# Two attention layers and two expert layers on one core: four groups of two heads in a turn of the loop instead of two

## The chip, the cores and the metric

The kernel runs on one core of a Trainium2 chip. The metric is the device time of one execution in microseconds (us). Before the change, three timed runs took 4503.47, 4507.40 and 4507.76 us, so the median is 4507.4 us. One further execution was profiled; it took 4508.5 us, and its trace spans 4506.7 us from the first to the last instruction.

## The reference, cut to what matters

The input x has 1024 rows of 128 numbers, and the context has 6404 rows of 128. Two layers follow each other, and each is a cross attention with 16 heads of 64 and then a mixture of 8 experts:

```python
x = x + tanh(g_xattn[0]) * xattn0(ctx, layernorm(x), mask, ...)   # keys: context and the 1024 rows; rmsnorm of q and k
x = x + tanh(g_ffn[0])   * moe0(layernorm(x), ...)
x = x + tanh(g_xattn[1]) * xattn1(layernorm(x), ctx, ...)         # keys: context and one null key
x = x + tanh(g_ffn[1])   * moe1(layernorm(x), ...)
# in each attention: softmax(q k^T) v for every head, then the output matrix
```

Nearly all the work is in the two attentions: 1024 queries against 7428 keys in the first and 6405 in the second, for every head.

## The kernel before

The kernel is written by hand for the five engines: each engine has its own list of instructions, and semaphores alone order them between engines. PE (TensorE) multiplies, ACT (ScalarE) exponentiates and copies, DVE (VectorE) forms the low parts of split numbers and adds outputs up, POOL (GpSimd) computes a few small roots, and SP (SyncE) issues the transfers.

`attention_layer` runs once for each of the two layers. The 16 heads go in `NG = 8` groups of `GH = 2` heads. Within a group the keys go in tiles of 128, which stand in ten chunks (59 tiles in the first layer, 51 in the second); each chunk is gone through twice, once for each half of the queries. One such step is one tile of keys by 512 queries by two heads. Steps go in pairs `i = 0 .. NPR - 1`, 59 and 51 pairs for a group.

In each pair PE computes the scores of two steps that lie ahead (L1114, three products for a split of 32-bit numbers into a high and a low part), then the outputs of the two present steps from the high part of the probabilities (L1132) and from the low part (L1139). ACT takes the exponential of the scores (`exp`, L638 in the first layer, L642 in the second), and DVE subtracts the high part from it (`p_low`, L797). Between these stand the projection of later tiles of keys and values (`project_kv`, L1049; `transpose_k`, L1057), what ACT and DVE make of it (`read_kv`, L607 and L609; `k_high`, L618; `v_wide`, L624; `v_low`, L781 and L783; `k_low`, L789), and the sums of outputs at the end of a chunk (`add_out`, L810). The output matrix of the group before and the queries of the group to come are spread over the pairs of a group as well.

Work runs over from one group into the next without a pause: the last pair of a group already computes the scores of the next group's first steps. Near the start of a group ACT copies the last sum rows (`e_high`, L693) and the output weights (`wo_split`, L657 and L658); near the end of one it splits the new queries (`q_high`, L680).

What matters here is how the eight groups are looped over. Each of the five engines has a counted loop of its own in each layer, over `NG // 2 = 4` turns, and a turn holds the instructions of two groups one after the other: groups 0 and 1, 2 and 3, 4 and 5, 6 and 7. A turn ends with a register operation and a compare-and-branch: PE's at L1161, ACT's at L729, DVE's at L976, POOL's at L590, SP's at L536. The branch is taken three times in a layer (from group 1 to 2, from 3 to 4, from 5 to 6) and falls through after the last. From group 0 to 1, 2 to 3, 4 to 5 and 6 to 7 an engine reads on straight ahead. What depends on the group's number (semaphore thresholds, rows of weights) is computed from the loop's register as `two * 2 + odd`.

Of the kernel before, what the change touches and what calls it, by code (L numbers as in the profile page):

```python
# [41 lines left out]
NG = H // GH  # L42
# [142 lines left out]
def attention_layer(nc, A, L, sem_, sb_, layer_norm, rstd, B):  # L185
# [25 lines left out]
    with scope:  # L211
# [288 lines left out]
        def place(k):  # L500

            k = k % NI
            c = max(c for c in range(NCH) if ITEM0[c] <= k)
            return c % 2, k - ITEM0[c]
# [3 lines left out]
        with nc.Block() as block:  # L508
            @block.sync
            def _(sp):  # L510
                def load_kv(r):
                    sp.dma_start(wkv_raw[:, :], A[NAME + "wkv_g"][bass.ds(r, 1), :, :].rearrange("a p n -> p (a n)")).then_inc(wkv_in, 16)

                def load_q(r):
                    sp.dma_start(wq_raw[:, :], A[NAME + "wq_g"][bass.ds(r, 1), :, :].rearrange("a p n -> p (a n)")).then_inc(wq_in, 16)

                def load_o(r):
                    sp.wait_ge(ql_done, 2 * r + 2)
                    sp.dma_start(wo_raw[:, :], A[NAME + "wo_g"][bass.ds(r, 1), :, :].rearrange("a p n -> p (a n)")).then_inc(wo_in, 16)
                    sp.dma_start(fin, A[NAME + "we_g"][bass.ds(r, 1), :, :].rearrange("a p n -> p (a n)")).then_inc(wo_in, 16)  # L520

                def load_den(r):
                    sp.wait_ge(o_added, 2 + r * NADD)
                    sp.dma_start(den_row.unsqueeze(0), oacc[P - 1:P, :, :]).then_inc(den_out, 16)
                    sp.wait_ge(den_out, 16 * (r + 1))
                    sp.dma_start(sums[:, 0, :], den_row.rearrange("h (p x) -> (h p) x", x=GH * NQ // P)).then_inc(sum_in, 16)
                    sp.wait_ge(den_rec, r + 1)
                    sp.dma_start(inv_row.rearrange("h (p x) -> (h p) x", x=GH * NQ // P), sums[:, 1, :]).then_inc(inv_out, 16)
                    sp.wait_ge(inv_out, 16 * (r + 1))
                    sp.wait_ge(c_ready, r + 1)  # L530
                    sp.dma_start(den[:, :, :], inv_row.partition_broadcast(P)).then_inc(den_in, 16)
                    sp.wait_ge(den_in, 16 * (r + 1))

                load_kv(0)
                load_q(0)
                with sp.Fori(0, NG // 2) as two:  # L536
                    for odd in range(2):
                        g = two * 2 + odd
                        load_o(g)
                        load_den(g)  # L540
                        sp.wait_ge(wkv_lo, g + 1)
                        load_kv(g + 1)
                        sp.wait_ge(wq_lo, g + 1)
                        load_q(g + 1)
                        if L == 1:
                            sp.wait_ge(v_ready, (g + 1) * NI)
                            r_ = CTX_REST
                            wide = [1, GH, P - 1]
                            sp.dma_start(v16[r_:r_ + 1, LASTP, T_LAST, :, 0:P - 1],
                                         null16[0:1, 0:P - 1].unsqueeze(1).broadcast_to(wide)).then_inc(null_in, 16)  # L550
                            sp.dma_start(v32[r_:r_ + 1, LASTP, T_LAST, :, 0:P - 1].bitcast(F32),
                                         null32[:, 0:P - 1].bitcast(F32).unsqueeze(1).broadcast_to(wide)).then_inc(null_in, 16)
                            for h in range(GH):
                                sp.dma_start(vlast[r_:r_ + 1, LASTP, T_LAST, h, 4:5], null16[0:1, P - 1:P]).then_inc(null_in, 16)
                load_o(NG)
                load_den(NG)

            @block.gpsimd
            def _(pool):
                step = Steps(pool, consts)  # L560
                step(nc.gpsimd.memset(oacc[:, :, :], 1.0))
                step(nc.gpsimd.memset(vlast[:, :, :, :, :], 0.0))
                step(nc.gpsimd.memset(v16[:, :, :, :, P - 1], 1.0))

                def k_rstd(k0, k):
                    if QK_NORM:
                        par, j = place(k)
                        pool.wait_ge(kn_var, k0 + k + 1)
                        nc.gpsimd.tensor_tensor(krs[:, par, 2 * j:2 * j + 2, :].rearrange("p t h -> p (t h)"), kst[:, 1, :],  # L569
                                                mhalf[:, 0:2 * GH], ALU.pow).then_inc(kn_rstd, 1)  # L570

                def q_root(r):
                    if QK_NORM:
                        pool.wait_ge(q_var, r + 1)
                        nc.gpsimd.tensor_tensor(qst[:, 2, :], qst[:, 1, :], mhalf[:, 0:QT * GH], ALU.pow).then_inc(q_rstd, 1)

                def bound(r):
                    pool.wait_ge(c_in_, r + 1)
                    pool.sem_inc(passed, 1)
                    nc.gpsimd.partition_all_reduce(call[:, :], cmx[:, :], P, RMAX).then_inc(c_all, 1)  # L580
                    pool.wait_ge(c_all, r + 1)
                    nc.gpsimd.tensor_tensor(call[:, 0:1], call[:, 0:1], phalf[:, 0:1], ALU.pow).then_inc(c_pow, 1)

                q_root(0)
                for k in range(2):
                    k_rstd(0, k)
                bound(0)
                for k in range(2, HEAD + 1):
                    k_rstd(0, k)
                with pool.Fori(0, NG // 2) as two:  # L590
                    for odd in range(2):
                        g = two * 2 + odd
                        for i in range(NPR):
                            if i in LOAD:
                                k_rstd(g * NI, LOAD[i][1])
                            if i == Q_ROW[1] + 1:
                                q_root(g + 1)
                            if i == Q_ROW[1] + 6:
                                bound(g + 1)

            @block.scalar
            def _(act):
# [123 lines left out]
                for n2 in range(2):  # L726
                    exp(0, 0, n2)
                read_kv(0, HEAD)
                with act.Fori(0, NG // 2) as two:  # L729
                    for odd in range(2):  # L730
                        g = two * 2 + odd
                        k0, s0 = g * NI, g * NS
                        for i in range(NPR):
                            if i == NPR - 1:
                                act.wait_ge(p_ready, s0 + NS)
                                bias_set(g + 1)
                            exp(s0, k0, 2 * i + 2)
                            items(g, i, "s")
                            exp(s0, k0, 2 * i + 3)
                            if i == 0:  # L740
                                e_high(g)
                            if i < GH:
                                o_high(g, i)
                            if i == 2:
                                wo_split(g)
                            if i == Q_ROW[0] - 2:
                                wq_split(g + 1)
                            if i in Q_ROW:
                                q_rows(g + 1, Q_ROW.index(i))
                            if i == Q_ROW[1]:  # L750
                                q_square(g + 1)
                            if i == Q_ROW[1] + 4 and QK_NORM:
                                q_square_again(g + 1)
                            if i in Q_COL:
                                q_cols(g + 1, Q_COL.index(i))
                            if i == NPR - 3:
                                q_high(g + 1, 0)
                            if i == NPR - 2:
                                q_high(g + 1, 1)
                            items(g, i, "me")  # L760
# [6 lines left out]
            def _(dve):  # L767
# [205 lines left out]
                    p_low(0, n2)  # L973
                v_low(0, HEAD)
                k_var(0, HEAD)
                with dve.Fori(0, NG // 2) as two:  # L976
                    for odd in range(2):
                        g = two * 2 + odd
                        k0, s0 = g * NI, g * NS
                        for i in range(NPR):  # L980
                            p_low(s0, 2 * i + 2)
# [52 lines left out]
            def _(pe):  # L1034
# [123 lines left out]
                project_kv(0, HEAD, 0, QSIDE0 if HEAD == 2 else None)  # L1158
                for n2 in range(2):
                    score(0, 0, 0, n2)  # L1160
                with pe.Fori(0, NG // 2) as two:  # L1161
                    for odd in range(2):
                        g = two * 2 + odd
                        k0, s0 = g * NI, g * NS

                        def item(i, slot):
# [321 lines left out]
```

## Time and profile before

| | |
|---|---|
| median of three runs | 4507.4 us (4503.47 to 4507.76) |
| the profiled execution | 4508.5 us, span 4506.7 us |
| PE busy | 4199.3 us, 93% of the span |
| DVE busy | 3411.4 us, 76% |
| ACT busy | 3192.4 us, 71% |
| POOL busy | 414.8 us, 9% |
| mean granted clock of PE | 0.972 |
| loop of the first layer | about 117 to 2292 us |
| loop of the second layer | about 2568 to 4403 us |

### The profile page before, as it was taken

The numbers are of one execution on the slowest core, as the hardware profiler recorded it, in microseconds if no ns is written. First come the engines' busy times: TensorE is split into PE (matmuls) and PEld (weight loads), VectorE is DVE, ScalarE is ACT, GpSimd is POOL, SyncE is SP. The second block draws the span as 40 slices with busy tenths as digits, with TensorE's granted clock in tenths as the row PEclk, the third lists the DMA queues.
The fourth block names the chain that finished last, engine by engine and source line by source line (L and its number), as shares of the span: only waits on it lengthen the run. The fifth ranks groups of instructions, "written<-read, shape, count | busy, mean of one in ns | idle before, by whom it ended". The sixth has DMA issues, their size and how long they took to land. (4 is left out here: it accounts for less than half of the span.)

```text
span 4506.7 us, 75798 instructions
## 1 busy us (share of the span) xinstructions
PE 4199.3 (93%) x26651; PEld 2695.9 (60%) x26651; DVE 3411.4 (76%) x5067; ACT 3192.4 (71%) x5163; POOL 414.8 (9%) x348
## 2 busy tenths in 40 slices
PE   2999999999999999999978499999999999999995
PEld 1556666666666656666646366666666666666663
DVE  5788878787887888788752577777777777777785
ACT  2788888888888888888842367676766666666661
POOL 4111111111111111111100000000000000000000
PEclk9999999999999999999989599999999999999996
DMA  1000000000000000000010000000000000000000
GB/s 36 16 1 16 1 5 12 1 16 1 17 1 1 16 1 17 1 5 12 1 51 25 26 3 14 3 5 12 5 12 5 12 5 12 2 15 1 16 1 23
DMA packets 27285, 48.16 MB, mean 11 GB/s; under 512 B 9329, under 2 KB 18425, under 8 KB 24313
## 3 DMA queue, kind: packets, MB, share of 16 engines
q1 hardware_dynamic: 24824, 42.30, 2.8%
q8 instruction: 237, 3.88, 0.4%
q14 instruction: 158, 1.29, 0.1%
q10 hardware_dynamic: 2066, 0.69, 0.1%
HBM read 42.15 MB, written 0.82 MB: 10 GB/s over the span
## 5 line engine op out<-in xcount | busy, mean ns | idle before, releaser
L797 DVE TENSOR_TENSOR a_probs_lo<-a_probs 128x1024 fp32r<-128x1024 f32 x1764 | 2119.5, 1223 | 656.8 <-ACT a_probs L642 306.8
L638 ACT ACTIVATE a_probs<-scores_ps,a_c_bias,a_k_rstd 128x512 f32<-128x512 f32 x1892 | 1317.2, 776 | 35.9 <-PE scores_ps L1114 34.4
L1139 PE MATMUL out_ps<-a_probs_lo,a_v 128*128 128x512 f32 x3520 | 1135.6, 443 | 0.0
L1132 PE MATMUL out_ps<-a_probs,a_v 128*128 128x512 bf16 x3520 | 968.7, 391 | 37.7 <-DVE a_out_acc L810 27.7
L642 ACT ACTIVATE a_probs<-scores_ps,a_c_bias 128x1024 f32<-128x1024 f32 x818 | 870.4, 1112 | 115.6 <-PE scores_ps L1114 114.6
L1114 PE MATMUL scores_ps<-a_q_hi,a_k_hi 64*128 64x512 f32 x3528 | 793.6, 445 | 18.3 <-issue 9.4
L1139 PEld LDWEIGHTS out_ps<-a_probs_lo,a_v 128*128 128x128 f32 x3520 | 659.2, 188 | 220.4 <-issue 0.3
L1114 PE MATMUL scores_ps<-a_q_lo,a_k_hi 64*128 64x512 f32 x3528 | 703.4, 393 | 0.0
L1114 PE MATMUL scores_ps<-a_q_hi,a_k_lo 64*128 64x512 f32 x3528 | 699.2, 391 | 0.0
L1132 PEld LDWEIGHTS out_ps<-a_probs,a_v 128*128 128x128 f16 x3520 | 273.8, 97 | 590.8 <-issue 222.9
L607 ACT ACTIVATE a_v<-proj_ps 128x256 f16<-128x256 f32 x456 | 175.5, 385 | 519.2 <-PE proj_ps L1049 519.0
L1114 PEld LDWEIGHTS scores_ps<-a_q_hi,a_k_hi 64*128 64x128 f32 x3528 | 333.2, 184 | 209.1 <-issue 109.6
L569 POOL TENSOR_TENSOR a_k_rstd<-a_k_stat,minus_half 128x4 f32<-128x4 f32 x244 | 301.5, 1236 | 1698.5 <-DVE a_k_stat L774 1698.5
L1114 PEld LDWEIGHTS scores_ps<-a_q_lo,a_k_hi 64*128 64x128 f32 x3528 | 336.0, 185 | 76.0
L810 DVE TENSOR_TENSOR a_out_acc<-out_ps,a_out_acc 128x512 f32<-128x512 f32 x576 | 369.1, 682 | 11.4 <-PE out_ps L1139 11.4
L1114 PEld LDWEIGHTS scores_ps<-a_q_hi,a_k_lo 64*128 64x128 f32 x3528 | 335.6, 186 | 37.5
L618 ACT ACTIVATE a_k_hi<-proj_ps 128x256 fp32r<-128x256 f32 x454 | 175.2, 386 | 248.6 <-PE proj_ps L1057 248.1
L624 ACT ACTIVATE a_v<-a_v 128x512 fp32r<-128x512 f16 x454 | 283.9, 625 | 0.0
L1122 PE MATMUL spare_ps<-a_probs,a_v_last 128*32 128x512 bf16 x3520 | 283.1, 395 | 0.0
L1049 PE MATMUL proj_ps<-a_wkv_hi,a_x_hi 128*128 128x256 f32 x912 | 267.4, 293 | 14.7 <-ACT normed_T L675 6.9
L1049 PE MATMUL proj_ps<-a_wkv_lo,a_x_hi 128*128 128x256 f32 x912 | 258.9, 284 | 0.0
L1049 PE MATMUL proj_ps<-a_wkv_hi,a_x_lo 128*128 128x256 f32 x912 | 257.0, 282 | 0.0
(198 smaller groups left out, 3431.1 us busy)
## 6 DMA issues: line engine op xcount, KB each, us to landing
a_den<-a_inv_row SPq DMA_DIRECT2D x18, 1024.0 KB, 4.7
normed<-in_L_xattn_we_g SPq DMA_DIRECT2D x18, 256.0 KB, 2.8
a_wkv_raw<-in_L_xattn_wkv_g SPq DMA_DIRECT2D x18, 128.0 KB, 2.0
a_wo_raw<-in_L_xattn_wo_g SPq DMA_DIRECT2D x18, 128.0 KB, 2.0
m_w<-in_L_ffn_w1T SPq DMA_DIRECT2D x1, 2048.0 KB, 8.2
m_w<-in_L_ffn_w2T SPq DMA_DIRECT2D x1, 2048.0 KB, 12.6
a_wq_raw<-in_L_xattn_wq_g SPq DMA_DIRECT2D x18, 64.0 KB, 1.9
residual<-in_x SPq DMA_DIRECT2D x1, 512.0 KB, 3.8
```

What stands on the lines that cost most here:

```text
L569: nc.gpsimd.tensor_tensor(krs[:, par, 2 * j:2 * j + 2, :].rearrange("p t h -> p (t h)"), kst[:, 1, :], mhalf[:, 0:2 * GH], ALU.pow).then_i ...
L607: nc.scalar.activation(v16[:, par, 2 * j:2 * j + 2, :, 0:DH].rearrange("p t h d -> p (t h) d"), proj[:, 2 * P:4 * P].rearrange("p (a d) -> ...
L624: nc.scalar.activation(v32[:, par, 2 * j:2 * j + 2, :, :].rearrange("p t h k -> p (t h) k"), v16[:, par, 2 * j:2 * j + 2, :, :].rearrange( ...
L638: ins = nc.scalar.activation(probs[:, pb, e * 512:(e + 1) * 512], scores[:, b, e * 512:(e + 1) * 512], ACT.Exp, bias=cbias[:, tile:tile + ...
L642: ins = nc.scalar.activation(probs[:, pb, :], scores[:, b, :], ACT.Exp, bias=cbias[:, 1:2] if last else cbias[:, 0:1])
L797: nc.vector.tensor_tensor(plow[:, idx % NPL, :], probs[:, idx % NB, :], p_hi[:, idx % NB], ALU.subtract).then_inc(plo_ready, 1)
L810: ins = nc.vector.tensor_tensor(oacc[:, e, q], outs[:, e * 512:(e + 1) * 512], oacc[:, e, q], ALU.add)
L1049: last = nc.tensor.matmul(dst, a[:, x], w[:, :].rearrange("p (a c) -> p a c", a=2), start=t == 0 and m == 0, stop=m == 2, skip_group_check ...
L1114: last = nc.tensor.matmul(scores[:, b, e * 512:(e + 1) * 512], kk[r, c % 2, t, :], qq[r, n * 512:(n + 1) * 512], start=m == 0, stop=m == 2)
L1122: last = nc.tensor.matmul(last_ps[j:j + 32, :], vlast[:, c % 2, t, e, 4 - 4 * n:36 - 4 * n], p_hi[:, idx % NB, e * 512:(e + 1) * 512], sta ...
L1132: nc.tensor.matmul(outs[:, e * 512:(e + 1) * 512], v16[:, c % 2, t, e, :], p_hi[:, idx % NB, e * 512:(e + 1) * 512], start=t == 0, stop=False)
L1139: nc.tensor.matmul(outs[:, e * 512:(e + 1) * 512], v32[:, c % 2, t, e, :], plow[:, idx % NPL, e * 512:(e + 1) * 512], start=False, stop=t ...
```

## The change

Each engine's loop makes `NG // 4 = 2` turns instead of 4, and a turn holds the instructions of four groups instead of two. The group's number is now `four * 4 + sub`. The same three lines change in each of the five loops; all else, the steps of a group included, stands as it was.

```diff
-                with pe.Fori(0, NG // 2) as two:
-                    for odd in range(2):
-                        g = two * 2 + odd
+                with pe.Fori(0, NG // 4) as four:
+                    for sub in range(4):
+                        g = four * 4 + sub
```

The same edit stands in the loops of `sp`, `pool`, `act` and `dve`. In each layer the taken branches from group 1 to 2 and from group 5 to 6 are gone, and the one from 3 to 4 stays. The loops' code is twice as long; the instructions that are executed are the same apart from the loop's own.

On PE, in the first layer, the end of the second group before the change. `proj_ps` is the projection's accumulator; L1161 is the loop:

```order
L1139 MATMUL out_ps<-a_probs_lo,a_v 128x512 x4
L1037 REGISTER_ALU
L1049 MATMUL proj_ps<-a_wkv_hi,a_x_hi 128x2x128
L1049 MATMUL proj_ps<-a_wkv_lo,a_x_hi 128x2x128
L1049 MATMUL proj_ps<-a_wkv_hi,a_x_lo 128x2x128
L1049 MATMUL proj_ps<-a_wkv_hi,a_x_hi 128x2x128
L1049 MATMUL proj_ps<-a_wkv_lo,a_x_hi 128x2x128
L1049 MATMUL proj_ps<-a_wkv_hi,a_x_lo 128x2x128
L1161 REGISTER_ALU
L1161 COMPARE_AND_BRANCH
```

The branch goes back to the loop's top, where the scores of a group's second pair ahead (L1114) are the first matrix work. After the change the same place, from the second group to the third, reads:

```order
L1049 MATMUL proj_ps<-a_wkv_hi,a_x_hi 128x2x128
L1049 MATMUL proj_ps<-a_wkv_lo,a_x_hi 128x2x128
L1049 MATMUL proj_ps<-a_wkv_hi,a_x_lo 128x2x128
L1103 ISA
L1107 ISA
L1114 MATMUL scores_ps<-a_q_hi,a_k_hi 128x512 x2
L1114 MATMUL scores_ps<-a_q_hi,a_k_lo 128x512 x2
L1114 MATMUL scores_ps<-a_q_lo,a_k_hi 128x512 x2
L1103 REGISTER_ALU
```

The two rows of the loop are gone, and two register operations of the next group's thresholds stand between its matrix work and the last projection. On DVE, before, the second group ended with the sum of outputs, the low part of the values, the statistics of the keys and the branch of L976:

```order
L810 TENSOR_TENSOR a_out_acc<-out_ps,a_out_acc 128x512
L778 REGISTER_ALU
L781 SCALAR_TENSOR_TENSOR a_v_last<-a_v,proj_ps 128x4
L783 SCALAR_TENSOR_TENSOR a_v<-a_v,proj_ps 128x4x63
L771 TENSOR_REDUCE a_k_stat<-normed 128x4
L774 TENSOR_SCALAR a_k_stat<-a_k_stat 128x4
L976 REGISTER_ALU
L976 COMPARE_AND_BRANCH
```

and after the change it reads on into the third group's first low parts of the probabilities:

```order
L771 TENSOR_REDUCE a_k_stat<-normed 128x4
L774 TENSOR_SCALAR a_k_stat<-a_k_stat 128x4
L794 ISA
L797 TENSOR_TENSOR a_probs_lo<-a_probs 128x1024
L794 REGISTER_ALU
L797 TENSOR_TENSOR a_probs_lo<-a_probs 128x1024
L890 TENSOR_TENSOR a_o_lo<-a_out_acc,a_o_hi 128x1024
```

No engine's other work changes its place.

## Rows read from the trace of the kernel before

**Rows 1.** The page: busy time, share of the span, instructions of each engine.

```profile
PE 4199.3 (93%) x26651; PEld 2695.9 (60%) x26651; DVE 3411.4 (76%) x5067; ACT 3192.4 (71%) x5163; POOL 414.8 (9%) x348
```

**Rows 2.** Source line L1161, PE's loop: whole span, then its first and second layer.

```profile
L1161 PEldq COMPARE_BRANCH  x8: 83/3881/4690, 667.5 to 4402.7; - x8
...
L1161 PEldq COMPARE_BRANCH  x3: 3497/3838/3924, 667.5 to 1750.0; - x3
...
L1161 PEldq COMPARE_BRANCH  x3: 4221/4476/4690, 3026.1 to 3942.6; - x3
```

**Rows 3.** Waits of PE: engine, line, waited for: us in total, times, longest.

```profile
PE scores_ps L1114 <- issue: 9.4, 6, 2.0
```

**Rows 4.** Timeline of PE from group 1 to 2: start, duration, what, idle before.

```profile
669.90 0.28 PE L1049 MATMUL proj_ps<-a_wkv_hi,a_x_lo 128*128 128x256 f32 x1
671.26 0.50 PE L1114 MATMUL scores_ps<-a_q_hi,a_k_hi 64*128 64x512 f32 x2 [1.09 <-issue]
...
675.34 0.50 PE L1114 MATMUL scores_ps<-a_q_hi,a_k_hi 64*128 64x512 f32 x2 [0.26 <-ACT a_probs L638]
...
676.68 0.50 PE L1114 MATMUL scores_ps<-a_q_hi,a_k_hi 64*128 64x512 f32 x2 [0.38 <-ACT a_probs L638]
```

**Rows 5.** Timeline of ACT, the same stretch.

```profile
670.90 0.42 ACT L613 ACTIVATE normed<-normed 128x256 f32<-128x256 f32 x1
673.84 2.79 ACT L638 ACTIVATE a_probs<-scores_ps,a_c_bias,a_k_rstd 128x512 f32<-128x512 f32 x4 [2.52 <-PE scores_ps L1114]
```

**Rows 6.** Timeline of DVE, the same stretch.

```profile
673.36 0.17 DVE L774 TENSOR_SCALAR a_k_stat<-a_k_stat 128x4 f32<-128x4 f32 x1
676.41 2.36 DVE L797 TENSOR_TENSOR a_probs_lo<-a_probs 128x1024 fp32r<-128x1024 f32 x2 [2.88 <-issue]
```

**Rows 7.** First layer, from the second L680 of a group to the next L657, seven crossings.

```profile
core 0: us, PE busy (x) PEld busy (x) DVE busy (x) ACT busy (x) POOL busy (x), PEclk, DMA share, GB/s
396.02:414.41 18.39, 17.89 (x114) 11.47 (x114) 16.07 (x25) 17.60 (x33) 2.95 (x2) 1.00 0.09 24
665.02:686.04 21.02, 19.03 (x118) 11.54 (x116) 16.13 (x25) 17.71 (x33) 2.00 (x2) 1.00 0.09 24
...
1205.59:1226.47 20.88, 18.68 (x118) 11.55 (x116) 15.82 (x25) 17.72 (x33) 1.86 (x2) 1.00 0.09 24
...
1747.57:1768.44 20.87, 19.00 (x118) 11.65 (x116) 16.04 (x25) 17.70 (x32) 2.00 (x2) 1.00 0.09 24
```

**Rows 8.** The same stretches of the second layer.

```profile
2794.47:2812.65 18.18, 17.70 (x112) 11.39 (x112) 14.98 (x21) 14.62 (x22) 0.00 (x0) 1.00 0.09 24
3023.07:3042.37 19.30, 17.49 (x112) 11.39 (x112) 15.17 (x21) 14.38 (x22) 0.00 (x0) 1.00 0.09 25
...
3481.45:3500.52 19.07, 17.51 (x112) 11.37 (x112) 15.17 (x21) 14.39 (x22) 0.00 (x0) 1.00 0.09 26
...
3939.55:3960.61 21.06, 19.03 (x112) 12.09 (x112) 15.26 (x21) 14.67 (x22) 0.00 (x0) 0.92 0.08 23
```

**Rows 9.** Timeline of PE in group 5 of the first layer, before L1132.

```profile
1607.83 0.40 PE L1132 MATMUL out_ps<-a_probs,a_v 128*128 128x512 bf16 x1 [1.47 <-DVE a_out_acc L810]
```

**Rows 10.** Stretches about that place in groups 0, 1 and 5.

```profile
255.50:262.50 7.00, 6.09 (x32) 3.27 (x33) 3.94 (x6) 2.61 (x6) 0.37 (x1) 0.76 0.00 0
526.80:533.80 7.00, 6.80 (x44) 3.95 (x46) 4.23 (x9) 4.00 (x8) 1.24 (x1) 1.00 0.00 0
1607.20:1614.20 7.00, 6.17 (x33) 3.39 (x34) 3.86 (x5) 2.61 (x7) 0.37 (x1) 0.76 0.00 0
```

**Rows 11.** Whole groups 3 and 5 of the first layer, from L693 to L693.

```profile
945.50:1216.90 271.40, 265.75 (x1715) 168.24 (x1713) 219.65 (x334) 228.83 (x404) 43.08 (x34) 1.00 0.02 8
...
1486.00:1758.90 272.90, 267.11 (x1715) 168.90 (x1713) 219.68 (x334) 228.84 (x404) 42.44 (x34) 0.99 0.02 7
```

**Rows 12.** The page: queues that fetch instructions: packets, MB, share of 16 engines.

```profile
q8 instruction: 237, 3.88, 0.4%
q14 instruction: 158, 1.29, 0.1%
```

More of the change, by code:

```diff
@@ L535, in _ @@
                 load_q(0)
-                with sp.Fori(0, NG // 2) as two:
-                    for odd in range(2):
-                        g = two * 2 + odd
+                with sp.Fori(0, NG // 4) as four:
+                    for sub in range(4):
+                        g = four * 4 + sub
                         load_o(g)
@@ L589, in _ @@
                     k_rstd(0, k)
-                with pool.Fori(0, NG // 2) as two:
-                    for odd in range(2):
-                        g = two * 2 + odd
+                with pool.Fori(0, NG // 4) as four:
+                    for sub in range(4):
+                        g = four * 4 + sub
                         for i in range(NPR):
@@ L728, in _ @@
                 read_kv(0, HEAD)
-                with act.Fori(0, NG // 2) as two:
-                    for odd in range(2):
-                        g = two * 2 + odd
+                with act.Fori(0, NG // 4) as four:
+                    for sub in range(4):
+                        g = four * 4 + sub
                         k0, s0 = g * NI, g * NS
@@ L975, in _ @@
                 k_var(0, HEAD)
-                with dve.Fori(0, NG // 2) as two:
-                    for odd in range(2):
-                        g = two * 2 + odd
+                with dve.Fori(0, NG // 4) as four:
+                    for sub in range(4):
+                        g = four * 4 + sub
                         k0, s0 = g * NI, g * NS
@@ L1160, in _ @@
                     score(0, 0, 0, n2)
-                with pe.Fori(0, NG // 2) as two:
-                    for odd in range(2):
-                        g = two * 2 + odd
+                with pe.Fori(0, NG // 4) as four:
+                    for sub in range(4):
+                        g = four * 4 + sub
                         k0, s0 = g * NI, g * NS
```

## The prediction

> **What bounds the kernel now.** I read the busy times first: PE works 93% of the span, and DVE and ACT, the next two, 76% and 71% [rows 1]. So a change moves the end only if it moves PE, or makes PE wait. The edit touches only the loops' ends, so the second view is that of the source line of PE's loop. Its branch stands eight times, four in each layer. The shortest is the one that falls through, 83 ns; the three taken ones of the first layer last 3.5 to 3.9 us, those of the second 4.2 to 4.7 us [rows 2]. That is how long PE's sequencer has nothing to issue after it jumps back. The third view says what of it reaches the array: PE waits for "issue" before L1114 six times, 9.4 us in total and 2.0 at most [rows 3], and six is the number of taken branches in both layers together. The array had work queued when the jump began and does not stand still for all of it.
>
> The timeline from group 1 to 2 shows that the loss is more than PE's own gap. PE's last projection starts at 669.90 and the next scores at 671.26, after 1.09 us of idle time [rows 4]. ACT has reached its own branch by then: its last copy starts at 670.90, and the exponential starts at 673.84, after 2.52 us [rows 5]; the scores are named as what it waited for, but PE had begun them at 671.26 [rows 4], 2.6 us earlier, so I take most of that wait for ACT's own jump. DVE comes last: L774 starts at 673.36 and L797 at 676.41, 2.88 us of idle time that nothing but issue explains [rows 6]. As ACT is late, PE waits twice more, 0.26 and 0.38 us [rows 4]. So each engine pays its jump, one after the other, and the sum on PE is read best from a stretch that encloses all of it.
>
> I chose the stretch from the last splitting of queries (L680) to the splitting of the output weights (L657) on ACT, since both stand in every group, a few pairs on either side of the crossing. In the first layer it takes 18.39 us in each of the four crossings where the engines read straight ahead (one row stands for them), and 21.02, 20.88 and 20.87 us where they jump [rows 7]. In the second it is 18.18 us straight ahead, in its four, and 19.30, 19.07 and 21.06 with a jump [rows 8]. The work in these windows is the same, down to the straight crossings agreeing to a hundredth, so the difference is the price of a jump. The second layer pays less although PE's branch is longer there: ACT has slack (14.4 to 14.7 us busy of 19 against 17.7 of 21), and part of the gap is made up within the stretch. Its third jump is an exception: the granted clock in that window is 0.92, where the others have 1.00. After 2.0 us of standing still, the longest such wait [rows 3], PE ran a while at 1.2 GHz. That makes 21.06 of what would else be about 19.2.
>
> **The change part by part.** Removed are the jumps from group 1 to 2 and from 5 to 6 in each layer. For these crossings I put the straight price in place of the price with a jump:
>
> - first layer, 1 to 2: 21.02 - 18.39 = 2.63 us; 5 to 6: 20.87 - 18.39 = 2.48 us [rows 7];
> - second layer, 1 to 2: 19.30 - 18.18 = 1.12 us; 5 to 6: 21.06 - 18.18 = 2.88 us [rows 8].
>
> The sum is 2.63 + 2.48 + 1.12 + 2.88 = 9.11 us. The jump from 3 to 4 stays in each layer and keeps its 20.88 - 18.39 = 2.49 and 19.07 - 18.18 = 0.89 us. Of the 2.88 us some 1.9 are the low clock; without it that jump would have cost about 1.0, as its two neighbours did, and the sum would be 7.2 us. All of it lies on PE's path, as PE has no other cover for it: its busy time within the straight windows is 17.89 of 18.39 us.
>
> Added is nothing that is executed more often. The new order shows two register operations where the branch stood on PE, and these are the next group's thresholds, which a straight crossing has today. They are issued while the array works off its queue, so I take them at nothing; were they not covered, they could not cost more than the straight windows already contain. The jumps of SP and POOL go as well. SP's next transfer waits on the queries' low part anyway, and POOL is busy 9% [rows 1], so I count nothing there.
>
> The code of a loop is twice as long. What that costs the trace does not show directly, so I bound it. Instructions come over two queues that carried 3.88 and 1.29 MB [rows 12]; at 75798 executed instructions that is some 68 bytes for each, so already now no turn finds its code still present, and every instruction is fetched anew in each turn. A longer turn then costs 0, which I take. From the other side, the wait after a jump could grow with the length of what is jumped over; the rows speak against it, because the first layer's turn is the longer one (59 pairs for a group against 51) and has the shorter branches, 3.5 to 3.9 against 4.2 to 4.7 us [rows 2]. If it doubled nevertheless, see the third rival.
>
> On the branch itself the rows say 3.5 to 4.7 us when taken and 83 ns when not [rows 2]. The Trainium skill, "Advanced Engine Details and Errata", section "Control Flow Timing", puts a compare-and-branch at about 108 ns; by that, four removed jumps would be worth an estimated 0.4 us, and the time would not change measurably. The trace agrees only for the branch that falls through. The skill's "Runtime: NRT & Kernel Launch", section "Instruction fetch mechanics", says that prefetch is sequential and that a jump out of its window stalls until the target has come; the trace shows such a stall, in the sizes named above.
>
> The sum is made against the profiled execution's own 4508.5 us (span 4506.7), which gives 4499.4. That execution lies 1.1 us above the median of the runs, 4507.4; from the median it is 4498.3. As the median is what counts, and as the low clock after one jump may not have been in every run, I take 4498.5 us.
>
> **What blurs it.** In the first layer PE waits 1.47 us for an output sum at the same place in every group [rows 9]. After it the clock fell in groups 0 and 5 (0.76 over 7 us) and not in group 1 [rows 10]; group 6 reads like 5, and the other four like 1. A group with the fall is 272.90 - 271.40 = 1.5 us longer [rows 11]. Whether it falls appears to hang on a coincidence in time, so between none and eight of these may occur, and three did: from -4.5 to +7.5 us at the very ends, and much less usually. The runs of before, from 4503.5 to 4507.8, show what such things sum up to.
>
> **The rivals.**
>
> - *The gain is taken back.* PE's queue hides the jump, and the time shows up as a wait for DVE or ACT later in the group. For it: in the second layer part of each gap is already made up within the stretch. Against it: the straight windows include the way to L657 and are shorter by all that I count. If only PE's own idle time at the four crossings counts in the first layer and nothing in the second, 1.1 us [rows 4] and 1.6 us (the mean of the 9.4 us over six waits [rows 3]) are gained, and the time is 4507.4 - 2.7, about 4505. By the skill's figure above it would be 4507.
> - *More low clock.* The crossings move all later groups in time, and five or more of the eight places in the first layer fall to the low clock where three did, 1.5 us each: five more than now cost 7.5 us, and the time is about 4506. Nothing speaks for it but that the place is on the edge in every group.
> - *Slower: the remaining jumps cost much more.* The wait at a jump grows with the body on every engine. If PE's 3.8, ACT's 2.5 and DVE's 2.9 us all double, and are paid one after the other, each remaining jump costs 9.2 us more, 18.4 in both layers; less the 9.1 gained, the time is 4507.4 + 9.3, about 4517. It decides from a point where each of the two remaining jumps costs over 9 us more than now ((9.1 gained + 9.0 to be told) / 2); below 4.6 us it is still a gain. Against it is that the longer layer has the shorter branches [rows 2].
>
> **How the numbers follow.** About 0.2% of the time, 9.0 us, is what a measurement of this kernel can tell from no change, so the line for faster is 4498.4 us. The forecast gets 0.80, and it lies on that line: the full 9.1 us is just over it, 7.2 is under it, and luck with the clock moves it by more than that. I split it into 0.44 faster and 0.36 within. The first rival gets 0.07 and the second 0.07, both within 0.2%; the slower one gets 0.06. Together: faster 0.44, same 0.50, slower 0.06. The range goes from 4494.4, the lowest run of before less 9.1, to 4503.4, the profiled execution less the 5.1 us of the first layer alone.
>
> **What would show it.** PE's branch should stand four times, two of them taken, at 3.5 to 4.7 us, and L1114 should wait for issue twice. The stretches from L680 to L657 should take 18.39 and 18.18 us from group 1 to 2 and 5 to 6, and still about 20.9 and 19.1 from 3 to 4. If the branch that stays is much above 5 us, the third rival is right; if the crossings are straight and the groups longer elsewhere at a clock of 1.00, the first; if they are longer at a lower clock, the second. The prediction is wrong in its base if a straight crossing in the new place costs more than 18.4 us.

## The result: 0.18% faster, and the time where it was expected

Over 21 runs of each kernel the median went from 4506.5 us (4500.6 to 4510.2) to 4497.6 us (4494.4 to 4504.9). The ratio is 0.9982, with a 95% interval of 0.9975 to 0.9988. The forecast was 4498.5 us, in a range of 4494.4 to 4503.4. The profiled execution of the changed kernel took 4498.6 us, its trace spans 4496.6.

The interval of the ratio stands for a gain of 5.4 to 11.3 us. The prediction had put its line between faster and the same at 9.0 us and given 0.44 to faster and 0.50 to the same; the measured 8.9 us lies just short of the line, and on which side it fell is chance.

### The profile after

PE's branch (the view of line L1161; durations in ns, shortest, median and longest) and its wait for issue (the view of waits) answer to [rows 2, 3]:

```profile
L1161 PEldq COMPARE_BRANCH  x4: 82/1805/4378, 1204.1 to 4392.3; - x4
```

```profile
PE scores_ps L1114 <- issue: 2.8, 2, 1.7
```

Four branches instead of eight, two of them taken, and two waits for issue instead of six: 9.4 us of PE's idle time there became 2.8.

The stretches from L680 to L657 answer to [rows 7, 8]. The columns are again the stretch, its length, the busy time of PE, PE's weight loads, DVE, ACT and POOL, then the granted clock. First layer, groups 0 to 1, 1 to 2, 3 to 4 and 5 to 6:

```profile
392.86:411.26 18.40, 17.90 (x114) 11.47 (x114) 16.08 (x25) 17.61 (x33) 2.95 (x2) 1.00 0.08 24
661.87:680.25 18.38, 17.88 (x114) 11.51 (x114) 16.07 (x25) 17.60 (x32) 2.94 (x2) 1.00 0.09 24
1201.58:1222.48 20.90, 18.89 (x118) 11.59 (x116) 15.96 (x25) 17.71 (x32) 2.00 (x2) 1.00 0.10 24
1743.55:1761.94 18.39, 17.89 (x114) 11.51 (x114) 16.07 (x25) 17.60 (x32) 2.94 (x2) 1.00 0.08 24
```

Second layer, 1 to 2, 3 to 4 and 5 to 6:

```profile
3016.61:3034.78 18.17, 17.69 (x112) 11.39 (x112) 14.98 (x21) 14.61 (x22) 0.00 (x0) 1.00 0.08 23
3473.88:3493.09 19.21, 17.49 (x112) 11.36 (x112) 15.17 (x21) 14.38 (x23) 0.00 (x0) 1.00 0.10 25
3932.12:3950.30 18.18, 17.70 (x112) 11.39 (x112) 14.99 (x21) 14.60 (x23) 0.00 (x0) 1.00 0.09 23
```

The four crossings that had a jump went from 21.02, 20.87, 19.30 and 21.06 us to 18.38, 18.39, 18.17 and 18.18: 9.13 us less. The two jumps that stay cost what they did, 20.90 for 20.88 and 19.21 for 19.07 us. That leaves a gain of 8.97 us at the crossings.

The spans differ by 10.1 us, 1.1 more. Group 0 of the first layer (from the L680 ahead of it to its own) accounts for 3.1 us, first of before, then of after:

```profile
112.86:396.02 283.16, 269.62 (x1698) 170.78 (x1698) 220.19 (x338) 230.17 (x408) 41.79 (x36) 0.98 0.02 7
```

```profile
112.83:392.86 280.03, 267.18 (x1697) 169.49 (x1697) 220.16 (x338) 229.85 (x407) 43.39 (x36) 0.99 0.02 7
```

Before, the clock fell once in this group [rows 10] and also stayed lower for longer at its start (a mean of 0.50 and 0.93 in the two stretches of 7 us from 127 us on); after, it did not fall in the group and was low more briefly (0.66 and 1.00). This is no gain of the change: a second trace of the same changed kernel took 282.4 us for group 0, 2.4 us more than the first. Later the changed kernel has three falls of 1.5 us where the old one had two, all at the same kind of place as in [rows 9, 10], now in groups 3, 4 and 7:

```profile
1062.00:1069.00 7.00, 6.80 (x36) 3.85 (x36) 3.49 (x6) 2.58 (x7) 0.37 (x1) 0.76 0.00 0
1335.00:1342.00 7.00, 6.80 (x36) 3.84 (x36) 3.49 (x6) 2.58 (x7) 0.37 (x1) 0.76 0.01 2
2144.00:2151.00 7.00, 6.80 (x37) 4.08 (x37) 3.50 (x7) 2.74 (x6) 0.37 (x1) 0.76 0.00 0
```

One small thing is given back. Groups that read on straight take 269.0 us from L680 to L680, but the third group of a turn takes 0.3 us more. Groups 1 and 2 of after:

```profile
392.86:661.87 269.01, 264.29 (x1706) 167.38 (x1705) 220.06 (x335) 228.80 (x404) 42.48 (x33) 1.00 0.02 7
661.87:931.14 269.27, 264.44 (x1706) 167.28 (x1705) 220.15 (x335) 228.89 (x405) 40.96 (x33) 1.00 0.02 7
```

Group 6, the third of the next turn, took 269.35 us, and the second trace of this kernel shows 269.34 and 269.33 us for the same two groups. The traces say where the time goes. Up to DVE's L774, 111.87 us after the L680 that opens the stretch, groups 1 and 2 run alike; then DVE's L797 starts at 111.97 us in group 1 and at 112.32 in group 2, and PE's next projection waits for the L789 behind it. Group 1, then group 2:

```profile
504.83 2.36 DVE L797 TENSOR_TENSOR a_probs_lo<-a_probs 128x1024 fp32r<-128x1024 f32 x2
...
774.19 2.36 DVE L797 TENSOR_TENSOR a_probs_lo<-a_probs 128x1024 fp32r<-128x1024 f32 x2 [0.28 <-ACT a_probs L638]
778.07 0.19 PEld L1049 LDWEIGHTS proj_ps<-a_wkv_hi,a_x_hi 128*128 128x128 f32 x1 [0.49 <-DVE a_k_lo L789]
```

The exponential that is named there runs no later in group 2 than in group 1. Why DVE starts late stays open.

### The profile page after: what moved, and what is told of

Its sections match the earlier page's. It is cut to its first block and busy times, and to the rows that moved or that the text cites. A ratio compares the mean times of both kernels' runs of the same rounds, so it can differ in the third digit from the quotient of the medians.

```text
span 4496.6 us, 75730 instructions
## 1 busy us (share of the span) xinstructions
PE 4196.5 (93%) x26651; PEld 2694.2 (60%) x26651; DVE 3411.4 (76%) x5067; ACT 3192.1 (71%) x5163; POOL 414.1 (9%) x348
## 5 line engine op out<-in xcount | busy, mean ns | idle before, releaser
L797 DVE TENSOR_TENSOR a_probs_lo<-a_probs 128x1024 fp32r<-128x1024 f32 x1764 | 2119.7, 1223 | 648.4 <-ACT a_probs L642 304.1
L1132 PE MATMUL out_ps<-a_probs,a_v 128*128 128x512 bf16 x3520 | 968.6, 390 | 39.5 <-DVE a_out_acc L810 29.8
L1114 PE MATMUL scores_ps<-a_q_hi,a_k_hi 64*128 64x512 f32 x3528 | 792.5, 445 | 9.9 <-ACT a_probs L638 6.7
L1114 PE MATMUL scores_ps<-a_q_lo,a_k_hi 64*128 64x512 f32 x3528 | 702.7, 393 | 0.0
L1114 PE MATMUL scores_ps<-a_q_hi,a_k_lo 64*128 64x512 f32 x3528 | 698.1, 390 | 0.0
L1132 PEld LDWEIGHTS out_ps<-a_probs,a_v 128*128 128x128 f16 x3520 | 273.7, 96 | 593.0 <-issue 220.5
L1114 PEld LDWEIGHTS scores_ps<-a_q_hi,a_k_hi 64*128 64x128 f32 x3528 | 332.7, 184 | 199.1 <-issue 101.8
L1114 PEld LDWEIGHTS scores_ps<-a_q_lo,a_k_hi 64*128 64x128 f32 x3528 | 335.1, 185 | 76.1
L810 DVE TENSOR_TENSOR a_out_acc<-out_ps,a_out_acc 128x512 f32<-128x512 f32 x576 | 369.2, 682 | 11.4 <-PE out_ps L1139 11.4
L1114 PEld LDWEIGHTS scores_ps<-a_q_hi,a_k_lo 64*128 64x128 f32 x3528 | 335.0, 186 | 37.8
```

The lines of the kernel that those rows point to most:

```text
L797: nc.vector.tensor_tensor(plow[:, idx % NPL, :], probs[:, idx % NB, :], p_hi[:, idx % NB], ALU.subtract).then_inc(plo_ready, 1)
L810: ins = nc.vector.tensor_tensor(oacc[:, e, q], outs[:, e * 512:(e + 1) * 512], oacc[:, e, q], ALU.add)
L1114: last = nc.tensor.matmul(scores[:, b, e * 512:(e + 1) * 512], kk[r, c % 2, t, :], qq[r, n * 512:(n + 1) * 512], start=m == 0, stop=m == 2)
L1132: nc.tensor.matmul(outs[:, e * 512:(e + 1) * 512], v16[:, c % 2, t, e, :], p_hi[:, idx % NB, e * 512:(e + 1) * 512], start=t == 0, stop=False)
```

## The experiments

Ten kernels ran. In all of them only the number of groups in a turn differs, for all engines or for some. The edit is always of this form, here for ACT:

```diff
-                with act.Fori(0, NG // 2) as two:
-                    for odd in range(2):
-                        g = two * 2 + odd
+                with act.Fori(0, NG // 4) as turn:
+                    for sub in range(4):
+                        g = turn * 4 + sub
```

### How many jumps, and how long a turn

All eight groups in one turn (`NG // 8`, all five engines):

> All eight groups in one turn of each loop, so no branch is taken in the loops at all. Theory 'jump' (each taken crossing costs what the stretch from L680 to L657 shows over a straight one, whatever the length of the turn): the last two crossings, 3 to 4, go from 20.9 to 18.39 us in the first layer and from 19.2 to 18.18 in the second; 3.5 us less than with four groups a turn, 12.6 less than with two, about 4494 us. Rival 'length' (a longer turn costs something of its own): no gain over four groups, or a loss, and the straight crossings above 18.39 and 18.18 us.

Measured: 4495.3 us (8 runs), ratio to before 0.9975, interval 0.9965 to 0.9986. Crossings from 3 to 4 in both layers:

```profile
1203.16:1221.55 18.39, 17.25 (x112) 11.40 (x114) 16.05 (x25) 17.61 (x32) 2.91 (x2) 1.00 0.09 24
...
3471.34:3489.55 18.21, 17.09 (x110) 11.37 (x112) 14.98 (x21) 14.60 (x22) 0.00 (x0) 1.00 0.09 24
```

No branch is taken, and these two crossings are straight as well. One of the first layer's (1 to 2) was 0.2 us longer than the rest, 18.59, and those of the second were 18.21 to 18.22 instead of 18.18; a longer turn costs no more than that there. Against the kernel before the median is 11.2 us lower, for 12.6 expected. It is 3.5 us below that of the changed kernel in the same comparison (below), as much as the two crossings cost, though the intervals of the two ratios overlap. This is the fastest version of the study.

One group in a turn (`NG // 1`, all five engines):

> One group in a turn, so seven taken branches in a layer, and a turn half as long as before. Theory 'jump': all seven crossings cost about 20.9 us in the first layer and 19.1 to 19.2 in the second, with PE's branch at 3.5 to 4.7 us as before; four jumps more in each layer, 4 x 2.5 + 4 x 1.0 = 14 us more than two groups a turn, about 4520 us, and a little more where the clock falls after a jump in the second layer. Rival 'length' (the wait grows with what is jumped over): PE's branch about half as long, 2 us, and less than 7 us more.

Measured: 4523.3 us (5 runs, 4517.8 to 4531.9), ratio 1.0040, interval 1.0027 to 1.0054. PE's branches in the first layer's loop and in the second's, seven each:

```profile
L1161 PEldq COMPARE_BRANCH  x7: 3527/3625/3890, 394.7 to 2025.4; - x7
...
L1161 PEldq COMPARE_BRANCH  x7: 4110/4350/4520, 2802.8 to 4182.0; - x7
```

These are about the durations of [rows 2] (3.5 to 3.9 and 4.2 to 4.7 us), although a turn is half as long, and 8 jumps more cost time, 16.8 us by the medians where 14 were expected. With turns of one, two and four groups the price of a jump is the same, and with eight no jump is taken; over these lengths it does not depend on how much is jumped over.

The changed kernel once more:

> The changed kernel once more, beside the two others: 8 to 9 us less than before, its straight crossings at 18.39 and 18.18 us. It is the measure for what one turn of eight groups adds.

Measured: 4498.8 us (11 runs), ratio 0.9981, interval 0.9972 to 0.9990. Its straight crossings took 18.38 to 18.39 and 18.18 us, its two jumps 21.00 and 19.09.

### Which engine's jump is the price

The next seven have four groups in a turn on some engines only. Each was run and traced once, so they are read by their stretches and not by their total times. ACT runs ahead of PE or behind it for a while after a crossing, so the stretch up to L657 can be short while PE is already late. I read a second stretch too, from L680 to the first L662 (the copy of the new queries), 68 us further on. In the kernel before it reads, first with a jump (1 to 2), then straight (2 to 3), in the first layer:

```profile
665.02:754.47 89.45, 86.54 (x553) 54.59 (x552) 73.19 (x111) 74.13 (x133) 9.99 (x9) 1.00 0.06 20
936.62:1023.43 86.81, 85.75 (x553) 54.74 (x552) 73.13 (x111) 74.02 (x132) 10.94 (x9) 1.00 0.07 20
```

So the price there is 2.64 us with all jumping, as much as at the near mark (2.63). In the second layer the straight stretch is 86.53 us. Of the rows behind each expectation the first is the crossing from 1 to 2 of the first layer up to L657, the next the same up to L662, the last the crossing from 1 to 2 of the second layer up to L657, unless the text says otherwise.

> Only PE's loop holds four groups in a turn; ACT, DVE, POOL and SP jump every two groups as before. Read from the stretch L680 to L657 at the crossings 1 to 2 and 5 to 6. Theory 'ACT sets the first layer's price' (ACT is busy 17.6 of 18.39 us there, and the scores run only 0.2 to 1 us ahead of it, so a delay of ACT's exponential by 2.5 us reaches PE nearly whole): about 20.7 to 21.0 us in the first layer, hardly better than 21.0 before; in the second, where ACT has room, 18.2 to 18.5. Rival 'PE's own gap is the price': the first layer falls to about 19.3 to 19.7.

```profile
663.58:684.36 20.78, 18.51 (x116) 11.51 (x116) 15.99 (x25) 17.72 (x33) 2.01 (x2) 1.00 0.09 23
...
663.58:752.78 89.20, 84.92 (x544) 54.54 (x552) 73.07 (x111) 74.12 (x132) 10.00 (x9) 1.00 0.06 20
...
3021.44:3039.76 18.32, 17.27 (x110) 11.54 (x112) 14.61 (x21) 14.09 (x22) 0.00 (x0) 1.00 0.09 25
```

PE's jump gone alone: hardly anything is won in the first layer, 0.2 us, and nearly all in the second. That fits the theory and not the rival; the next run shows that the theory is not the whole.

> Only ACT's loop holds four groups in a turn. Theory 'ACT sets the first layer's price': what stays is PE's own gap of 1.1 to 1.5 us, so the stretch takes 19.5 to 19.9 us in the first layer; in the second about 19.1, as before, because there PE's gap is the price. Rival 'PE's own gap is the price and ACT's jump hides behind it': no change in either layer, 20.9 and 19.1.

```profile
661.65:681.79 20.14, 17.60 (x112) 11.41 (x114) 15.37 (x25) 17.70 (x32) 1.41 (x2) 1.00 0.09 24
...
661.65:750.64 88.99, 84.37 (x544) 54.79 (x552) 72.86 (x111) 74.12 (x133) 9.99 (x9) 1.00 0.06 20
...
3018.97:3038.26 19.29, 17.16 (x110) 11.41 (x112) 15.18 (x21) 14.38 (x22) 0.00 (x0) 1.00 0.10 24
```

Neither foresaw this. The near stretch is 0.9 us shorter, but at L662 only 0.5 of 2.64 us are gone, 2.18 are left. ACT is not the only one that sets the price; something else holds most of it up.

> Only DVE's loop holds four groups in a turn. DVE's low parts of the probabilities are needed 2 us after they are made, and its jump of 2.9 us runs beside ACT's. Theory: no change, 20.9 to 21.0 and 19.1 us. Rival 'the jumps add up one after the other, DVE's last': 0.5 us or more less in the first layer.

```profile
661.67:682.66 20.99, 18.66 (x116) 11.48 (x116) 16.33 (x25) 17.69 (x33) 2.00 (x2) 1.00 0.09 23
```

No change, as the theory had it. In the second layer one crossing took 19.79 us, with a branch of PE of 4.94 us and a gap of 2.3 us behind it, and the other 19.18, with 4.33 and 1.7.

> PE and ACT hold four groups in a turn; DVE, POOL and SP jump every two. What stays is DVE's jump alone: L797 about 2.9 us late where PE has 2.1 to 2.7 us of room, so 0.3 to 1 us over a straight crossing: 18.7 to 19.4 us in the first layer, 18.2 to 18.7 in the second. If DVE's jump costs nothing, 18.39 and 18.18.

```profile
661.55:681.50 19.95, 17.75 (x112) 11.01 (x112) 15.18 (x25) 17.71 (x32) 1.23 (x2) 1.00 0.07 22
...
661.55:750.53 88.98, 84.70 (x544) 54.56 (x552) 72.86 (x111) 74.12 (x133) 9.99 (x9) 1.00 0.06 20
...
3015.72:3033.90 18.18, 17.13 (x110) 11.40 (x112) 14.90 (x21) 14.61 (x22) 0.00 (x0) 1.00 0.09 24
```

A miss in the first layer: with PE and ACT straight, 1.56 us are left at L657 and 2.17 at L662, not 0.3 to 1. In the second nothing is left. DVE's timeline and then PE's at the first layer's crossing show the way it takes:

```profile
669.89 0.17 DVE L774 TENSOR_SCALAR a_k_stat<-a_k_stat 128x4 f32<-128x4 f32 x1
672.94 2.36 DVE L797 TENSOR_TENSOR a_probs_lo<-a_probs 128x1024 fp32r<-128x1024 f32 x2 [2.87 <-issue]
675.22 1.22 DVE L890 TENSOR_TENSOR a_o_lo<-a_out_acc,a_o_hi 128x1024 fp32r<-128x1024 f32 x1
676.35 0.42 DVE L789 TENSOR_TENSOR a_k_lo<-proj_ps,a_k_hi 128x256 fp32r<-128x256 f32 x1
```

```profile
675.35 0.74 PE L1139 MATMUL out_ps<-a_probs_lo,a_v 128*128 128x512 f32 x2 [0.39 <-DVE a_probs_lo L797]
676.82 0.38 PE L1049 MATMUL proj_ps<-a_wkv_hi,a_x_hi 128*128 128x256 f32 x1 [0.73 <-DVE a_k_lo L789]
```

The expectation had counted the low parts of the probabilities alone. But DVE's list holds L890 and L789, the low part of the keys, behind them, and in this crossing both come 2.9 us later than in a straight one. PE's next projection waits for L789. Two later waits of PE for DVE's sums (L810 and L808 before L1132) are together 0.9 us longer than in a straight crossing; with the 0.39 and 0.73 us shown, that is 2.0 of the 2.17 us.

> PE, ACT and DVE hold four groups in a turn; only POOL and SP jump every two. With PE and ACT straight and DVE, POOL and SP jumping, 1.6 us of the first layer's price were left in the stretch L680 to L657, and 2.2 us up to the first L662 of the group. Theory: that was DVE's jump, so now 18.39 us in the first layer and 18.18 in the second, and 86.81 and 86.53 us from L680 to L662, as with everything straight. Rival: it was POOL's jump (the roots of the keys' norms are on the way to ACT's exponential): still 1.5 us or more over 18.39 in the first layer.

```profile
663.63:682.02 18.39, 17.89 (x114) 11.46 (x114) 16.08 (x25) 17.61 (x33) 2.95 (x2) 1.00 0.09 24
...
663.63:750.44 86.81, 85.77 (x553) 54.74 (x552) 73.14 (x111) 74.02 (x133) 10.94 (x9) 1.00 0.06 20
...
3014.53:3032.71 18.18, 17.70 (x112) 11.40 (x112) 14.98 (x21) 14.61 (x23) 0.00 (x0) 1.00 0.08 24
```

All of it is gone with PE, ACT and DVE straight. The jumps of POOL and SP cost nothing, as the prediction had it.

> ACT alone jumps every two groups, all others every four. Theory 'any one engine's jump costs the first layer nearly the whole price, so the prices do not add': 20.5 to 20.9 us in the stretch L680 to L657 and 2.2 to 2.5 us over a straight crossing up to L662 in the first layer; 18.2 to 18.4 us in the second, where ACT has room. Rival 'the prices add up': PE 1.1 to 1.5 plus ACT's share make 2.6, so ACT alone costs 0.3 to 1 us.

```profile
663.01:683.97 20.96, 19.25 (x118) 11.44 (x116) 16.31 (x25) 17.69 (x32) 2.00 (x2) 1.00 0.09 22
663.01:752.40 89.39, 86.75 (x553) 54.44 (x552) 73.35 (x111) 74.09 (x133) 9.99 (x9) 1.00 0.06 20
...
3021.03:3039.28 18.25, 17.77 (x112) 11.46 (x112) 14.61 (x21) 14.09 (x23) 0.00 (x0) 1.00 0.10 24
```

ACT's jump alone, with every other engine straight, costs the first layer 2.57 us at L657 and 2.58 at L662, nearly the whole 2.63 and 2.64, and the second layer 0.1 to 0.2. The prices do not add.

> PE alone jumps every two groups, all others every four. PE's own gap is then the whole price in both layers: 19.5 to 19.9 us in the first layer's stretch, 1.1 to 1.5 us over a straight crossing up to L662 too; 19.1 to 19.3 us in the second, the same as with all engines jumping, since there the others have room. If the first layer shows 2.5 us even so, PE's jump costs more than the gap that is seen before L1114.

```profile
1743.80:1764.23 20.43, 18.40 (x118) 11.76 (x116) 16.31 (x25) 17.70 (x32) 2.00 (x2) 1.00 0.09 23
1743.80:1832.67 88.87, 85.90 (x553) 54.78 (x552) 73.36 (x111) 74.13 (x133) 10.00 (x9) 1.00 0.06 20
3018.99:3037.98 18.99, 17.49 (x112) 11.36 (x112) 15.17 (x21) 14.38 (x23) 0.00 (x0) 1.00 0.08 24
```

PE's jump alone costs 20.43 - 18.39 = 2.04 us in the first layer (5 to 6; from 1 to 2 a stretch of low clock is in the 20.90 us), and 0.8 to 0.9 in the second. The second layer's stretches, 18.99 and 19.09 us, are close to the 19.1 to 19.3 expected. The first layer's is above the 1.1 to 1.5 expected, because the gap before L1114 was itself longer, 2.00 us at that crossing:

```profile
1750.95 0.50 PE L1114 MATMUL scores_ps<-a_q_hi,a_k_hi 64*128 64x512 f32 x2 [2.00 <-issue]
```

From 1 to 2 the gap was 1.88 us. PE's branches lasted 4.30 and 4.41 us at these two crossings, against 3.50 and 3.92 with all engines jumping, where the gaps were 1.09 and 1.50 us. So part of PE's price alone is a longer branch, and why it is longer no run shows.

The table sums it up, in us over a straight crossing at L662, from group 1 to 2 and from 5 to 6.

| engines that jump | first layer | second layer |
|---|---|---|
| all five (before) | 2.64, 2.52 | 1.12, 2.88 (low clock) |
| ACT, DVE, POOL, SP | 2.39, 2.47 | 0.27, 0.33 |
| PE, DVE, POOL, SP | 2.18, 2.31 | 1.11, 1.04 |
| PE, ACT, POOL, SP | 2.59, 2.46 | 1.61, 1.00 |
| DVE, POOL, SP | 2.17, 2.29 | 0.00, 0.00 |
| ACT | 2.58, 2.39 | 0.19, 0.25 |
| PE | 2.51 (low clock), 2.06 | 0.81, 0.91 |
| POOL, SP | 0.00, -0.01 | -0.01, -0.04 |

## Why the prediction was right, and where it was not

- **The price of a jump, from enclosing stretches.** Right. The four crossings fell by 9.13 us for the 9.11 forecast, and each came down to the straight stretch within 0.01 us. The two remaining jumps stayed within 0.14 us. That the same work had been timed with a jump and without one in the same trace made this possible.
- **The medians.** The measured difference is 8.9 us; the forecast took 8.9 off the median of the three runs. That these agree to 0.1 us is luck. The full 9.1 and the 7.2 without a fall of the clock can't be told apart: the runs of each kernel scatter over some 10 us, and both figures lie within the interval of 5.4 to 11.3. The 1.9 us of the fall were counted in full, though such a fall came after only 4 of the 25 jumps that PE made in the second layer over all traces of this study (a granted clock of 0.92 in the stretch each time). The two jumps removed there would by that share be worth an estimated 0.6 us of falls on average, about 7.8 us in all.
- **How the price comes about.** The text said that each engine pays its jump, one after the other. That was wrong for the costs, though the jumps do begin one after another, and the sum did not rest on it. In the first layer any one of the three costs 2.1 to 2.6 us alone, and all together 2.5 to 2.6. They overlap: a jump of one engine while another is late anyway adds little or nothing. In the second layer PE's jump alone costs 0.8 to 0.9 of the 1.1 us, which fits the slack of ACT that the prediction named.
- **What the longer turn costs.** Taken as nothing, and the wait after a jump does not grow with it. The 0.3 us in the third group of a turn of the first layer, 0.6 us in all, were not foreseen.
- **The first rival, the gain taken back,** is out: the stretch up to L662 is down by as much as the near one, to 86.81 and 86.80 us in the first layer of the changed kernel, the straight figure. Something like it does happen when the change is made on PE alone: PE's own gap is gone, and of the 2.64 and 2.52 us in the first layer only 0.25 and 0.05 are won.
- **The second rival, more low clock,** is out for the profiled run, three falls at that place against three, now in other groups. The second trace of the changed kernel has its falls in the same groups 3, 4 and 7, and over all traces the lengths of groups 1 to 7 show none to three such rises of 1.5 us. That fits a coincidence in time; no experiment tested it.
- **The slower rival** is out by the two jumps that stayed and by the runs with one and with eight groups in a turn. The compare-and-branch of about 108 ns of the Trainium skill, "Advanced Engine Details and Errata", section "Control Flow Timing", is near the one that falls through (82 ns here); PE's taken ones lasted 3.5 to 4.4 us in the changed kernel.

## What to carry to other kernels

Where a loop's turn holds several equal blocks, the trace already has each crossing with a jump and without; the difference over a stretch that encloses it is the price of a jump, and here it could be multiplied: 14 us forecast for eight jumps more, 16.8 measured. Do not add up the gaps of the engines: take the jump away from all engines that are near the critical path, because each one alone can hold nearly the whole price. Read such a price well behind the place as well, since a near mark on one engine may be early while the others are late.

## What the runs showed of the hardware

- A taken branch of PE's sequencer lasted 3.5 to 4.9 us, and its duration did not grow with the loop's body (one, two or four groups of some 270 us in the first layer and 230 in the second). PE itself stood still for 1.0 to 2.3 us of it; in the kernel before, the branch from group 1 to 2 began at 667.5 us and the matmuls already issued ran on until 670.2. On ACT a jump opened 2.5 us before the next instruction, on DVE 2.9. There the branch's own row does not show it: ACT's (L729) lasts 40 to 54 ns and DVE's (L976) 55 to 80 in the kernel before, taken or not, and the time stands as idle time before the next instruction:

```profile
668.90 0.42 ACT L613 ACTIVATE normed<-normed 128x256 f32<-128x256 f32 x1
671.79 1.45 ACT L638 ACTIVATE a_probs<-scores_ps,a_c_bias,a_k_rstd 128x512 f32<-128x512 f32 x2 [2.47 <-issue]
```

  These rows are from the kernel in which ACT alone jumps every two groups.
- A taken jump costs extra fetches. The queue q8 carried 237 packets with two groups in a turn, 229 with four and 253 with one, two of 16 KB for each jump of PE. It goes with PE's loop alone: 229 or 230 packets in every kernel where PE jumps every four groups, 237 in every one where it jumps every two. With one turn there are 215, fewer than the jumps account for, which fits the register operations that are gone with it (below). The row of the changed kernel:

```profile
q8 instruction: 229, 3.75, 0.4%
```

- Register operations for the thresholds cost nothing here that the stretches show. With one turn the trace has 66624 instructions instead of 75730 (75290 in the second trace of that kernel, so the count itself varies by some 440); the register operations of L1103, 1744 of them before, are gone from it. The crossings that were straight before did not get faster (18.39 and 18.21 us).
